# Experts stage as the tail of the middle stage's block: early loads into dead buffers, dispatch ahead of slot sums

## What is computed

```python
logits = (jnp.einsum('tzd,ed->tze', x, phi_w) + phi_b).reshape(t, z, n, p)
D = jax.nn.softmax(logits, axis=3)            # over the 32 slots of an expert
C = jax.nn.softmax(logits, axis=2)            # over the 64 experts
X_tilde = jnp.einsum('tznp,tzd->npd', D, x)   # dispatch, summed over all tokens
X_tilde = jnp.clip(X_tilde, -33000.0, 65000.0)
...
X_tilde = jnp.tanh(X_tilde)                   # after a layer norm over d
Y_tilde = jnp.einsum('npd,ndH->npH', X_tilde, expert_w) + expert_b[:, None, :]
Y = jnp.einsum('tznp,npH->tzH', C, Y_tilde)   # combine
...
x = x + attention(xn) + mixture(xn)
```

## Time and profile before

| | us |
|---|---|
| median of 3 runs | 1402.18 (1401.42 to 1403.56) |
| profiled execution, its own time | 1401.86 |
| its span, first to last instruction | 1399.8 |
| middle stage, about | 57 to 1211 |
| experts stage | 1211.3 to 1239.9 |
| combine | 1239.9 to 1399.8 |

### The profile page before, as it was taken

How to read it: one execution, slowest core, us unless ns; L and a number is a source line. 1 busy time by engine, 2 the same in 40 slices (tenths; PEclk the granted TensorE clock), 3 DMA queues, 4 the chain that set the end, 5 groups by cost and what they waited for, 6 DMA issues and landing times. The chain is left out here.

```text
span 1399.8 us, 28649 instructions
## 1 busy us (share of the span) xinstructions
PE 1329.0 (95%) x9520; PEld 1007.2 (72%) x9520; DVE 1112.0 (79%) x1932; ACT 1047.6 (75%) x3221; POOL 1098.1 (78%) x852
## 2 busy tenths in 40 slices
PE   2899999999999999999999999999999999469998
PEld 2677777777777777777777777777777777258887
DVE  7677888878877887788878877887788778658876
ACT  4678888888888888888888888888888888345554
POOL 2478878888888788888888888888888888559985
PEclk9999999999999999999999999999999999779999
DMA  5111121112111211122111211121111111487873
GB/s 171 44 52 67 67 71 68 67 67 78 69 67 67 65 59 67 67 76 71 67 61 65 79 69 67 67 78 69 67 46 65 63 65 39 143 242 255 260 252 128
DMA packets 99714, 126.25 MB, mean 90 GB/s; under 512 B 20080, under 2 KB 47728, under 8 KB 99440
## 3 DMA queue, kind: packets, MB, share of 16 engines
q1 hardware_dynamic: 95904, 122.97, 25.9%
q10 hardware_dynamic: 3664, 1.44, 0.4%
HBM read 48.89 MB, written 35.65 MB: 60 GB/s over the span
## 5 line engine op out<-in xcount | busy, mean ns | idle before, releaser
L676 ACT ACTIVATE e<-ps_s,neg_max 128x256 f32<-128x256 f32 (+1 forms) x1024 | 414.3, 430 | 133.2 <-DVE neg_max L748 133.2
L748 DVE TENSOR_REDUCE neg_max<-ps_s 128x2 f32<-128x512 f32 (+1 forms) x384 | 241.3, 684 | 136.8 <-PE ps_s L539 136.8
L887 POOL TENSOR_TENSOR disp<-logit,gmax 128x512 f32<-128x512 f32 x128 | 134.6, 1052 | 248.0 <-DVE gmax L790 248.0
L663 ACT ACTIVATE pT<-ps_t 128x512 f32<-128x512 f32 x384 | 239.7, 625 | 65.8 <-PE ps_t L514 65.2
L895 POOL TENSOR_TENSOR e<-e,inv 128x1024 f32<-128x1024 f32 x128 | 284.6, 2223 | 0.0
L514 PEld LDWEIGHTS ps_t<-ident,e 128*128 128x128 f32 x1536 | 186.2, 140 | 86.0 <-issue 65.7
L514 PE MATMUL ps_t<-ident,e 128*128 128x128 f32 x1536 | 230.1, 272 | 1.2 <-ACT pT L663 1.2
L676 ACT ACTIVATION_READ_ACCUMULATOR e<-ps_s,neg_max 128x1 f32 x1024 | 221.7, 217 | 0.0
L539 PEld LDWEIGHTS ps_s<-qk 64*128 64x128 f32 x2048 | 172.8, 186 | 44.5 <-issue 40.6
L539 PE MATMUL ps_s<-qk 64*128 64x256 f32 (+1 forms) x2048 | 202.4, 337 | 0.0
L1110 POOL TENSOR_TENSOR c_back<-c_back,c_inv 128x512 f32<-128x512 f32 x104 | 138.2, 1367 | 36.5 <-POOLq L925 30.0
(11 more groups left out here) (134 smaller groups left out, 2987.5 us busy)
## 6 DMA issues: line engine op xcount, KB each, us to landing
xs<-xT SPq DMA_DIRECT2D x128, 256.0 KB, 2.4
c_scratch<-logit SPq DMA_DIRECT2D x128, 256.0 KB, 2.0
c_back<-c_scratch SPq DMA_DIRECT2D x32, 1024.0 KB, 5.6
fx<-xT SPq DMA_DIRECT2D x64, 64.0 KB, 1.9
fxn<-xn SPq DMA_DIRECT2D x32, 64.0 KB, 2.0
xres<-in_L_attn_x SPq DMA_DIRECT2D x8, 256.0 KB, 6.0
out_dram<-res SPq DMA_DIRECT2D x8, 256.0 KB, 5.1
xn<-in_L_attn_x SPq DMA_DIRECT2D x2, 512.0 KB, 6.9
```

The source lines that it names most:

```text
L663: nc.scalar.activation(pT[:, k, :], ps_t[:, (q + k) % 2, :], ACT.Copy).then_inc(t_out, 1)
L676: ins = nc.scalar.activation(dst, ps_s[:, k, i * width:(i + 1) * width], ACT.Exp, bias=neg_max[:, q, c:c + 1], accum_out=total[:, q, c:c + 1])
L748: nc.vector.tensor_reduce(neg_max[:, q, c:c + heads], ps_s[:, k, :].rearrange("p (h t) -> p h t", h=heads), AX.X, ALU.max, negate=True).th ...
L887: nc.gpsimd.tensor_tensor(by_expert(bank_of(disp, t, jj)), by_expert(bank_of(logit, t, jj)), gmax[:, jj, :].unsqueeze(2).to_broadcast([P, ...
```

## The change

- The experts stage has no block of its own. Its instructions stand at the end of the middle stage's programs, so one barrier is gone. It works in PSUM banks and buffers that are free by then: transposes and products in `free_banks`, the slots in `qk[0]`, their transposes in `qk[1]`, `eb` in the even half of `disp`, `y_t` in `phiT`.
- Expert weights are loaded in eight pieces of 0.52 MB into the first halves of `xT` and into `xn`: seven after the last `fx` load, ahead of the last iteration's stores, the eighth after the last `fxn`. The first two `c_back` buffers are the other halves of `xT` and are loaded behind the seven pieces. `c_back` 2 and 3 are loaded at combine's start.
- PE makes `dispatch(31, 1)` ahead of the last `output`, and `times_wo(63)` after the last dispatch. The last tile's bank use is `j % 2`.
- On POOL, in the run-out, the dispatch scaling comes before the slot sums, and the slot sums of tile 31 move to DVE, behind the normalisation of the slots. POOL then scales `c_back` 0 and 1 inside the middle stage's block.
- `c_all` is inverted tile by tile: one reciprocal of 32 columns an iteration, in step j = 0 (`slot_inverse`), in place of one of 1024.
- The clip is done in four quarters.
- In combine DVE shares from group 2 on.

The diff, cut to its core (the experts stage's own instructions are moved as they were, with other buffers):

```diff
+        free_banks = [ps_s[:, 0, :], ps_s[:, 1, :], ps_s[:, 2, :], ps_t[:, 0, :]]
...
+        def xt_bank(t, j):
+            return j % 2 if t == LAST else BANKS[j]["xt"]
...
-            for it in range(ITER):
+            for it in range(ITER - 1):
                 iteration(it, it % PER, it // PER)
+            for q in range(2):
+                sp.wait_ge(xs_in[q], 16 * NU)
+            sp.wait_ge(fx_in, 32 * NTT)
...
+            for c in range(7):
+                load_experts(c)
+            for n in range(2):
+                load_weights(sp, env, n)
+            iteration(ITER - 1, (ITER - 1) % PER, (ITER - 1) // PER)
+            sp.wait_ge(fxn_in, 16 * NTT)
+            load_experts(7)
+            sp.wait_ge(xt_mm, 4 * LAST)
+            per_tile = env["expert_b"].rearrange("(t r) h -> r t h", r=4)
+            for r in range(4):
+                sp.dma_start(env["eb"][NP_ * r:NP_ * (r + 1)], per_tile[r].partition_broadcast(NP_)
+                             ).then_inc(env["eb_in"], 16)
             for n in range(4 * NTT - 6, 4 * NTT):
                 store_weights(n // 4, n % 4)
...
-                    if live(unit - 2, NU):
+                    if live(unit - 2, NU) and v != NV + 2:
                         times_wo(unit - 2, g - 1 if kk == 0 else g, use["wo"])
...
+                if v == NV + 1:
+                    dispatch(LAST, 1)
                 if live(v - 2, NV):
                     output(v - 2, (j + 2) % 4, unit - 1)
...
-                if live(it - 1, NTT):
+                if live(it - 1, NTT) and v != NV + 1:
                     dispatch(it - 1, j)
+                if v == NV + 3:
+                    times_wo(NU - 1, NG - 1, BANKS[2]["wo"])
...
+            def slot_inverse(t):
+                if live(t, NTT):
+                    dve.wait_ge(c_sum, t + 1)
+                    part = c_all[:, t * NP_:(t + 1) * NP_]
+                    nc.vector.reciprocal(part, part).then_inc(c_inv, 1)
...
                 if j == 3:
-                    slot_sum(it - 2)
+                    if it < ITER + 1:
+                        slot_sum(it - 2)
+                if j == 0:
+                    slot_inverse(it - 3)
...
+            take_wo(NU - 1, BANKS[2]["wo"])
             for c in range(NQ):
+                dve.wait_ge(xt_out, 4 * LAST + c + 1)
+                part = xt_acc[:, c * BK:(c + 1) * BK]
+                nc.vector.tensor_scalar(part, part, -33000.0, 65000.0, ALU.max, ALU.min).then_inc(clip_done, 1)
...
-            nc.vector.reciprocal(c_inv[:], c_all[:])
-            dve.wait_ge(eb_in, 64)
+            for j in range(1, 4):
+                dve.wait_ge(c_exp, 4 * LAST + j + 1)
+                wait(dve, c_bank, 3 * LAST + j - 1)
+                so_far = bank_of(logit, LAST, 0) if j == 1 else c_run[:]
+                nc.vector.tensor_tensor(c_run[:], so_far, bank_of(logit, LAST, j), ALU.add).then_inc(c_bank, 1)
+            slot_sum(LAST)
+            dve.wait_ge(env["eb_in"], 64)
...
+            for c in range(2):
+                pool.wait_ge(env["c_back_in"][c], 16)
+                for i in range(4):
+                    ins = normalise(nc.gpsimd, env, c, i)
+                ins.then_inc(env["by_pool"], 1)
...
+        def shares(c):
+            return 2 <= c < NG_ and c % 4 > 0
...
+            for n in range(2, NB_):
+                load_weights(sp, env, n)
             for n in range(NB_, 4 * NPAIR + NB_):
```

More of the change, by code:

```diff
@@ L55 @@
 ITER = NTT
+EW = NE // 8
 def wait(eng, sem, value):
@@ new lines, in expert_weights, with normalise @@
+def expert_weights(env, first, count):
+    place, at = env["ew"][first // EW]
+    at += (first % EW) * D
+    return place[:, at:at + count * D].rearrange("p (n d) -> p n d", d=D)
+def normalise(eng, env, c, i):
+    part = env["c_back"][c % len(env["c_back"])][:, i, :].rearrange("p (e s) -> p e s", s=NP_)
+    t = 4 * (c // 4) + i
+    return eng.tensor_tensor(part, part, env["c_all"][:, t * NP_:(t + 1) * NP_].unsqueeze(1)
+                             .to_broadcast([P, EB, NP_]), ALU.mult)
@@ L1100, in combine_phase @@
         NG_ = 4 * NPAIR
+        def shares(c):
+            return 2 <= c < NG_ and c % 4 > 0
         def shared(c):
-            return c - (c + 3) // 4
-        def normalise(eng, c, i):
-            part = c_back[c % NB_][:, i, :].rearrange("p (e s) -> p e s", s=NP_)
-            t = 4 * (c // 4) + i
-            return eng.tensor_tensor(part, part, c_inv[:, t * NP_:(t + 1) * NP_].unsqueeze(1)
-                                     .to_broadcast([P, EB, NP_]), ALU.mult)
+            return sum(shares(k) for k in range(c))
         block = ctx.enter_context(nc.Block())
@@ L1136, in _ @@
         def _(pool):
-            for c in range(NG_):
+            for c in range(2, NG_):
                 pool.wait_ge(c_back_in[c % NB_], 16 * (c // NB_ + 1))
-                for i in range(4 if c % 4 == 0 else 3):
-                    ins = normalise(nc.gpsimd, c, i)
+                for i in range(3 if shares(c) else 4):
+                    ins = normalise(nc.gpsimd, env, c, i)
                 ins.then_inc(by_pool, 1)
@@ L1269, in build @@
             main_phase(nc, env)
[L1270 to L1274 removed]
+        env["c_back"] += [sb(f"c_back{q}", [P, 4, BK])[:] for q in range(2, 4)]
         combine_phase(nc, env)
```

291 lines of the change are left out of this document (140 added, 151 removed).

## The result

The changed kernel takes 1394.87 us (median of 7 runs, 1390.81 to 1398.74), the kernel before 1402.89 (7 runs, 1401.42 to 1403.56): a ratio of 0.9945, 95% interval 0.993 to 0.996. That is 8 us gained where 10.5 were forecast, inside the range of 1386.5 to 1396.5, 3.4 above the forecast's 1391.5. The profiled execution took 1394.55 with a span of 1392.8.

A forecast was written before the change was run, and what follows sets the result against it. PE bounds the middle stage and combine; the change works on the 62 us between them, where PE is half idle. Terms of -7.6, -5.4, +1.7 and +0.8 sum to -10.5, giving 1391.5 us, range 1386.5 to 1396.5.

The forecast's parts named there:

- Clip earlier: Run-out: the last bank's clip, freed of the barrier and tile 31's POOL additions, comes at 1204.8 against 1211.31, -6.5 us.
- clip in quarters: Run-out: PE's first transpose waits for a quarter clip of about 0.35 us instead of 1.23, -0.9 us.
- first exponentials ready: Between DVE's last experts instruction and PE's combine start only a barrier is left of 5.74 us, -5.4 us.
- POOL works beside DVE: Experts stage: POOL's eight c_back scalings hold up DVE's clips and small layer norm operations, +3.5 us, bounds 0 and 3.6.
- Reciprocal in the loop: Middle stage: a 32-column reciprocal in each of 29 iterations, mostly swallowed by DVE's waits, costs +0.8 us, bounds 0 and 8.1.
- Transfers gone, `eb`: Experts stage: without the eb wait, DVE follows product by product, ending 7.2 us after the products' start, not 10.48; -3.3 us.
- The next two loads late: Combine: c_back 2 and 3, issued after the barrier, make PE wait after its first eight groups, +1.7 us, bounds 0 and 4.
- Early loads: Late middle stage: nine loads ahead of tile 29's stores drain in time, first store near 1178.7, needed at 1179.68; 0 us.
- stores late: Rival, chance 0.14: the load queue runs slower, DVE stalls some 4 us for a store, 1395.5 us.
- the slower rival: Rival, chance 0.06: the load queue falls to half of 290 GB/s, DVE stalls 21.8 us in iteration 31, 1413 us.
- reciprocal fully exposed: Rival, chance 0.08: all 29 loop reciprocals cost their full length, +7.3 us, 1398.8 us.
- Nothing holds DVE up: Rival, chance 0.20: POOL's scalings cost the layer norm only 0 to 1 us in place of 3.5, 1388.5 us.

The follow-up runs named there:

- e4: The changed kernel with POOL's old run-out order, slot sums ahead of dispatch scalings (tile 31's stay on DVE): 1395.21 us, ratio 0.9945.
- e2: The changed kernel with POOL's eight scalings of the first two c_back buffers held until DVE has normalised the slots: 1389.33 us, ratio 0.9905.
- e8: The changed kernel with the clip as one instruction of 2048 columns in place of four quarters: 1395.35 us, ratio 0.9935.
- e3: The changed kernel with c_back 2 and 3 loaded before the barrier, into the bias buffer and half of the dispatch buffer: 1393.16 us, ratio 0.993.
- e9: The kernel before with only the per-tile reciprocal of 32 columns added in step j = 0, in place: 1404.8 us, ratio 1.0011.
- e1: The changed kernel with the tile's reciprocal moved from DVE's step j = 0 to step j = 1: 1392.11 us, ratio 0.993.
- e12: The changed kernel with its long-lived buffers allocated in the order of the kernel before: 1392.29 us, ratio 0.992.
- e7: The changed kernel with e2's and e3's edits, slot_sum(30) and last o_acc addition later, three POOL subtractions held for the clips, last reciprocal earlier: 1388.81 us, ratio 0.9896.
- e10: The combination e7 with ACT's last three exponentials of the stored weights moved behind its four copies of transposed slots: 1383.55 us, ratio 0.9855.
- e11: The combination e10 plus 56 identity transposes on PE through the layer norm and an early one-column tanh on ACT: 1384.72 us, ratio 0.9866.

## Why the prediction was right, and where its size was off

*Clip earlier, clip in quarters, `ew`, first exponentials ready:* right within 0.3 us each. What the clip waits for was read correctly from the two orders: POOL's third addition of tile 30 and the slot sum behind it, in both orders (e4).

*POOL works beside DVE:* the mechanism is the one forecast, down to the clips held at one per POOL instruction and the second tensor-tensor ending with the eighth scaling. The size was 2.8 for 3.5, and e2 gives 2.9 with the scalings moved. The Trainium skill, "SBUF — State Buffer", section "SBUF: two separate sides", has a lock held for a whole instruction by whichever engine starts first; e2 and e8 agree, also in that the statistics, on one input, aren't slowed (3.18 us beside POOL, 3.43 without it in e2). What neither page nor prediction had is who comes next: DVE after one POOL instruction in the changed kernel, after eight in e3. The forecast's bound of 3.6 was too low by that draw: in e3 the second tensor-tensor ends 18.0 us behind the first clip's start, 9.9 more than in e2. And the prediction's "No row of before has a single-input SBUF instruction beside POOL" holds for tensor-scalars alone. The sums `dsum<-disp`, nearly all beside a POOL instruction, took 0.63 to 0.68 us in all 128 cases of before, so the trace already showed that one input in SBUF is not enough to be held.

*Reciprocal in the loop, +0.8:* the wrong mechanism with nearly the right size. The loop grew by 1.3 us in this trace, but e9 shows that the reciprocal costs nothing in the kernel before, because DVE's wait of 0.91 us in the next step swallows it; the prediction had looked only as far as the 0.16 us wait behind it. The growth begins in iterations 0 to 2, which hold no reciprocal (lag 1.24, 1.26, 1.30), and its cause is open after e1 and e12.

*Transfers gone, `eb`:* the waits went, but products to DVE's end gave 2.0 for 3.3. The step that failed is the one that kept the products at the 4.8 us of the earlier trace rows: PE ran most of them at clock 0.50 and they took 5.7 (1226.80 to 1232.5). The 4.8 were themselves a draw, since the second trace of before has 5.2. In e12 the clock came back early, the products took 4.4, and DVE ended 7.4 us behind their start, against the forecast's 7.2.

*The next two loads late, +1.7:* the wait was where it was put and 3.24 us long, within the bounds of 0 and 4, and longer than forecast because PE came early. The weights came 9.7 us after PE's start, as forecast (10.0), while PE was through its first eight groups after 6.5 and not 8.2: it ran them at clock 1.00, and the forecast took the first four from the earlier trace rows, run at 0.50. Against before, where the ninth group began 8.25 us after the start, the wait costs 1.45, close to the 1.7. The other 1.3 are a second price that I had only as a tail: the clock fell in the wait, so the ninth group's transposes took 1.11 us where four take 0.60 elsewhere. Together 2.8; e3 shows that early loads give all of it back, and 2 us more.

*Early loads, 0:* right, with the spare time that was forecast. In the changed kernel's trace the first store behind the loads has landed at 1181.24 (1178.7 with the lag of 2.57 taken off, the forecast's figure), 1.0 us ahead of the logits that need it. DVE's logits of iteration 31, step 2, wait for PE and not for a store, as in the earlier trace rows:

```profile
1182.25 0.69 DVE L869 TENSOR_TENSOR logit<-ps_tu,bias 128x512 f32<-128x512 f32 x1 [0.91 <-PE ps_tu L79]
```

So "stores late" and the slower rival, with the same place and more of it, did not come. The reciprocal fully exposed fell with e9. "Nothing holds DVE up" fell for the changed kernel with its clips of 4.81 us; e2's kernel, which takes the scalings away from the clips, comes near it at 1389.33 beside the rival's 1388.5.

*The baseline:* 1.2 us of the 3.5 between forecast and trace are setup, and no part of the change. They came in because all steps were summed against one execution, and that one had the shortest setup of all.

*The range:* the forecast's own bounds end at 1394.5, and the measured 1394.87 lies just above them. It is the width added for "stores late", which did not come, that holds it, so this much is luck.

## What to carry to other kernels

Work put on an idle POOL is not free for a DVE chain beside it: start it where DVE reads PSUM (e2's bias additions took 0.68 to 0.69 us, three of them beside POOL) or has cover, not beside clips and small tensor-tensors, where e2's one wait took the ratio from 0.9945 to 0.9905. Before a wait is put on one engine to spare another, follow what the waiting engine feeds, since its consumer may stand ahead of the critical work on a third engine (e7 against e10, 5.3 us in the medians, 3.9 at combine's start with lags taken off). And take the baseline of a sum from two traces, or at least check its setup, before terms of 1 us are argued.

## What the runs showed of the hardware that I had not expected

- Four DVE clips of 512 columns beside POOL's back-to-back instructions took 4.67 to 5.38 us in five traces (the changed kernel's two, e1, e4, e12) and 11.34 in e3; without POOL they took 1.42 (e2). In the changed kernel and in e3 alike the first was issued 0.3 us ahead of the end of a POOL instruction.
- Two executions of the same program differ by up to 1.64 us before the first tile. PE's granted clock, at 0.50 when the projections begin, comes back to 1.00 some 3 us earlier or later.
- The same wait at PE's ninth group (3.0 to 3.5 us) went with a fall of the granted clock to 0.50 in four traces (the changed kernel's two, e4, e8) and with none in e1.
- 56 transposes in PE's idle stretch did not carry the full clock to the products: it was 0.82 and then 0.50 in the 4 us stretches behind them (e11).
